# Layer 1: the network's first weight tiles fetched and split during the attention, and its first products in the steps of the last head group

## The chip, the core and the metric

The kernel runs on one core of one Trainium2 chip. The metric is the time of one execution on the device in microseconds (us), as the median of several runs. The engines are TensorE (PE; its weight loads are shown apart as PEld), VectorE (DVE), ScalarE (ACT), GpSimd (POOL) and SyncE (SP), which here only issues DMAs. Each works through a queue of its own in program order and waits on semaphores for the others.

## What is computed

Two transformer layers in float32 over S = 1024 tokens of width 512. The case touches only layer 1, and of it the end of the attention and the feed-forward network; both read the same normalised input `xn`:

```python
xn = _layernorm(x)
# grouped attention: H = 32 query heads of 16, G = 8 groups of 4 heads share keys and values
scores = einsum('bhqd,bhkd->bhqk', q, k); causal; weights = softmax(scores / sqrt(HD))
ctx = einsum('bhqk,bhkd->bhqd', weights, v)
attn = dot(ctx, Wo) + bo
# network: F = 2048
h = gelu(einsum('bsd,df->bsf', xn, inter_w) + inter_b, approximate=True)
out = einsum('bsf,fd->bsd', h, output_w) + output_b
x = x + attn + out
```

## The kernel before

**Products of float32 accuracy.** Most large products are made as three products of a faster type (`mm3`, lines 105 to 107): each operand is split into a high part (a cast by ACT) and a low part (operand less high part, a subtraction by POOL or DVE), and PE adds high x high, high x low and low x high into one PSUM bank. PSUM has 8 banks of 512 columns, `ps[:, 0]` to `ps[:, 7]`.

**Attention, `grouped_attention`.** Eight head groups g = 0 to 7, each of 12 steps (`STEPS`): four for the first 512 queries, eight for the last 512, one for each block of 128 keys. The width of a step is the number of queries that may look at the block: 512, 384, 256, 128, then 512 five times, 384, 256, 128. In a step PE makes the transposed scores of two pairs of heads (`keys`, line 1914, two products each, banks 0-1 and 2-3). ACT takes the exponential of each pair into `ga_pt` (line 1994). On the diagonal POOL masks a block (line 2032), and two steps later PE multiplies with the values (`weigh`, line 1930, eight instructions into bank 7). The scores of a bank pair may be written only when the exponential before has read it. Beside this, in each step, PE makes score products of the *next* group (line 1891, banks 4 to 6), and DVE their row maxima (line 1974), which give the shift of the softmax. The last group has no next one, so in its steps these products are missing. ACT copies the context out of bank 7 twice in a group (line 2007). SP writes it to memory, reads back its sums (`csum`, line 1766) and the context (line 1769); DVE inverts the sums (line 1795), SP writes these out (line 1777) and loads them spread out over partitions with eight DMAs (line 1788); POOL scales the heads with them (line 1802).

**Network, `heads_and_ffn`.** A new stage behind a barrier of all engines, with semaphores set anew. 16 tiles k of 128 hidden features. For each tile SP loads 256 KB of weights (`first`, line 2081, a ring of RW = 4 tiles), ACT makes the high part (`high1`, line 2148), POOL the low part (`low1`, line 2195). PE makes two halves of 512 tokens, 4 x 3 products each (`up`, 24 products for a tile, banks 2 * (k % 2) + half), and ACT applies bias and gelu (line 2159). `up(k)` waits for the low part of its tile, and from k = 2 for the gelu that frees the bank. Then `down` multiplies with the second weights and with Wo, 20 times, into all eight banks, and DVE adds x.

The order of the queues at the start of this stage, written out by hand:

- SP: tiles 0 and 1, b1, tiles 2 and 3; then for the last head group the sums, the context, the two bias vectors spread over partitions, the inverted sums out, the eight spread loads; then tile 4 and the others, each when its place in the ring is free.
- ACT: high parts of tiles 0 and 1; wait for b1; then for each k the high part of tile k + 2 and the two gelus of tile k.
- POOL: low parts in order of k; behind that of tile 4 the sum of the two biases (line 2207) and eight additions of it to x (line 2210); behind that of tile 6 the scaling of the last heads.

```python
for k in range(NC):
    low1(k)
    if k == 4:
        pool.wait_ge(bias_in, START + 32)
        pool.tensor_tensor(bias[:, 0], bias[:, 0], bias[:, 1], ALU.add).then_inc(bias_done, 1)
        ...
        for t in range(ST):
            pool.tensor_tensor(x[:, t], x[:, t], bias[:, 0], ALU.add).then_inc(x_ready, 1)
```

`outputs_to_queries` is the stage ahead of the attention (projections of layer 1). It has a weight buffer `oq_w` of two tiles and high parts `oq_wh` of six blocks of 128 columns.

Of the kernel before, what the change touches and what calls it, by code (L numbers as in the profile page):

```python
# [13 lines left out]
P = 128  # L14
# [1415 lines left out]
def outputs_to_queries(nc, c, ps, ident, x, ctx_d, wvo_d, xnh, xnl, wq, wkv, qkd, v32, ctxn, raw, sums, qst, kst, q_in,  # L1430
                       k_in, strip, nmax, nT, first):
# [26 lines left out]
    with ExitStack() as st:  # L1458
        cf = Ctx(nc, st)
        w = cf.sb("oq_w", [P, 2, DT, P])  # L1460
        wh = cf.sb("oq_wh", [P, DT, NW], F32R)
# [26 lines left out]
        with nc.Block() as block:  # L1488
# [41 lines left out]
            @block.gpsimd  # L1530
            def _(pool):
                def low_block(n):
                    pool.wait_ge(wh_done, START + n + 1)
                    at = slice(BLOCKS[n] * P, (BLOCKS[n] + 1) * P)
                    pool.tensor_tensor(wl[:, :, at], w[:, n % 2], f32(wh[:, :, at]), ALU.subtract).then_inc(wl_done, 1)

                for half, k, s, u in steps:
                    pool.wait_ge(split_done[s], START + u + 1)
                    pool.tensor_tensor(ol_w[:, s], wr[:, s], f32(oh_w[:, s]), ALU.subtract).then_inc(wvl_done[s], 1)
                    if (half, k) in SPLIT_AT:  # L1540
                        low_block(SPLIT_AT[half, k])
                    if (half, k) == (0, 5):
                        pool.memset(v32[:, :, :, HD1:], 1.0).then_inc(ones_done, 1)
                    if (half, k) == (0, 7):
                        pool.memset(f32(kst[:, :, 1]), 0.0).then_inc(zero_b, 1)
                        pool.wait_ge(zero_b, START + 1)
                        pool.memset(f32(kst[KQ1:KQ1 + 2, :, 1]), 1.0).then_inc(zero_b, 1)
                        pool.wait_ge(zero_b, START + 2)
                        pool.memset(f32(kst[KQ1:KQ1 + 1, :, 1]), 0.0).then_inc(zero_b, 1)
                        pool.wait_ge(zero_b, START + 3)  # L1550

            @block.scalar
            def _(act):
# [9 lines left out]
                def high_block(n):  # L1563
                    act.wait_ge(w_in[n % 2], START + LANDED[n])
                    at = slice(BLOCKS[n] * P, (BLOCKS[n] + 1) * P)
                    act.copy(wh[:, :, at], w[:, n % 2]).then_inc(wh_done, 1)
# [128 lines left out]
            def _(pe):  # L1695
# [20 lines left out]
                def task(n):  # L1716
# [9 lines left out]
                    for k in range(DT):  # L1726
                        if kind == "T":
                            a1, a2 = slice(m * P, (m + 1) * P), slice(h * HALF, (h + 1) * HALF)
                            ins = mm3(pe, ps[:, n % 4, :], (wh[:, k, a1], wl[:, k, a1]), (xnh[:, k, a2], xnl[:, k, a2]),
                                      k == 0, k == DT - 1)  # L1730
                            if k == DT - 1:
                                ins.then_inc(done, 1)
                        else:
                            a1 = slice(m * P, (m + 1) * P)
                            ins = mm3(pe, ps[:, n % 4, 0:KD], (xnh[:, k, a1], xnl[:, k, a1]),
                                      (wh[:, k, D + KD:], wl[:, k, D + KD:]), k == 0, k == DT - 1)
# [67 lines left out]

def grouped_attention(nc, ps, ident, strip, qkd, raw_d, inv_d, v32, ctxn, qst, kst, q_in, k_in, rest, nmax, nT,
                      first):
# [26 lines left out]
    with ExitStack() as st:  # L1833
# [12 lines left out]
        with nc.Block() as block:  # L1846
            @block.sync
            def _(sp):
# [16 lines left out]
                for g in range(G1):  # L1865
# [7 lines left out]
                    if g + NB < G1:  # L1873
                        load(g + NB)
                store(G1 - 1, 1)

            @block.tensor
            def _(pe):
# [59 lines left out]
                for g in range(G1):  # L1938
                    done = lead
                    for s in range(NSTEP):  # L1940
                        ahead = g + 1 if s < NSTEP - LEAD else g + 2
                        first = done if s < NSTEP - LEAD else done - UNITS
                        units = range(first, first + SHARE[s]) if ahead < G1 else range(0)
# [3 lines left out]
                        for v in units[:one]:  # L1947
                            score(ahead, v)
                        keys(g, s, 1)
                        for v in units[one:two]:  # L1950
                            score(ahead, v)
# [4 lines left out]
                        for v in units[two:]:  # L1956
                            score(ahead, v)
# [28 lines left out]
            def _(act):  # L1986
# [22 lines left out]
                for g in range(G1):  # L2009
                    for s in range(NSTEP):  # L2010
# [6 lines left out]
                        if s == 3 + LAG:  # L2017
                            take_ctx(g, 0)
                take_ctx(G1 - 1, 1)

            @block.gpsimd
            def _(pool):
                for g in range(G1):
                    for s, (half, j) in enumerate(STEPS):
                        off, q0, q1 = span(half, j)
                        if q0 == j * P:
                            n = g * NSTEP + s
                            for p in range(2):
# [4 lines left out]
                                               channel_multiplier=-1, compare_op=ALU.is_ge, fill=0.0).then_inc(sel_done, 1)  # L2033
                    if g >= 3 and g % 2 == 1:
# [4 lines left out]
def heads_and_ffn(nc, ps, xnh, xnl, x, ctxn, raw_d, inv_d, rest, wo, bo, w1, b1_d, w2, b2_d, out_d):  # L2039
# [5 lines left out]
    with ExitStack() as st:  # L2045
        c = Ctx(nc, st)
        g = c.sb("t_g", [P, NC, S])
        w1r = c.sb("t_w1r", [P, RW, DT, P])
        w1h = c.sb("t_w1h", [P, RW, DT, P], F32R)
        w1l = c.sb("t_w1l", [P, RW, DT, P], F32R)  # L2050
# [7 lines left out]
        names = ("b1_in", "bias_in", "bias_done", "x_ready", "w1h_done", "w1l_done", "w2h_done", "w2l_done", "hidden",  # L2058
                 "h_done", "gh_done", "gl_done", "used", "summed", "x_done", "stored")
        (b1_in, bias_in, bias_done, x_ready, w1h_done, w1l_done, w2h_done, w2l_done, hidden, h_done, gh_done, gl_done,  # L2060
         used, summed, x_done, stored) = (c.sem("t_" + n) for n in names)
        w1_in, w2_in = c.sems("t_w1_in", RW), c.sems("t_w2_in", RW)
        w1_v = w1.rearrange("(k p) n -> p k n", p=P)

# [10 lines left out]
        with nc.Block() as block:  # L2075
            @block.sync
            def _(sp):
                def first(k):
                    if k >= RW:
                        sp.wait_ge(w1l_done, START + k - RW + 1)  # L2080
                    sp.dma_start(w1r[:, k % RW], w1_v[:, :, k * P:(k + 1) * P]).then_inc(w1_in[k % RW], 16)
# [7 lines left out]
                first(0)  # L2089
                first(1)  # L2090
                sp.dma_start(b1[:, :], b1_d.rearrange("(k p) -> p k", p=P), allow_slow_non_contiguous=True).then_inc(b1_in, 16)
                first(2)
                first(3)
                for half in (1,):
# [15 lines left out]
            def _(pe):  # L2110
                def up(k):
                    pe.wait_ge(w1l_done, START + k + 1)
                    for half in range(2):
                        tok = slice(half * HALF, (half + 1) * HALF)
                        if k >= 2:
                            pe.wait_ge(h_done, START + 2 * (k - 2) + half + 1)
                        for j in range(DT):
                            ins = mm3(pe, ps[:, 2 * (k % 2) + half, :], (w1h[:, k % RW, j], w1l[:, k % RW, j]),
# [18 lines left out]
                for k in range(NC):  # L2137
                    up(k)
# [4 lines left out]
            def _(act):  # L2143
                def high1(k):
# [3 lines left out]
                    act.copy(w1h[:, k % RW], w1r[:, k % RW]).then_inc(w1h_done, 1)  # L2148
# [7 lines left out]
                def activate(k):  # L2156
                    for half in range(2):
                        act.wait_ge(hidden, START + 2 * k + half + 1)
                        act.activation(g[:, k, half * HALF:(half + 1) * HALF], ps[:, 2 * (k % 2) + half, :],
# [13 lines left out]
                high1(0)  # L2173
                high1(1)
# [17 lines left out]
            def _(pool):  # L2192
                def low1(k):
                    pool.wait_ge(w1h_done, START + k + 1)
                    pool.tensor_tensor(w1l[:, k % RW], w1r[:, k % RW], f32(w1h[:, k % RW]), ALU.subtract).then_inc(  # L2195
# [7 lines left out]
                for k in range(NC):  # L2203
# [68 lines left out]
def two_layers(nc, ins, consts, out):  # L2272
# [9 lines left out]
    with ExitStack() as top:  # L2282
# [44 lines left out]
        with ExitStack() as layer1:  # L2327
# [9 lines left out]
            for name in ("raw_out", "sum_in", "ctx_in", "scale_in"):  # L2337
                rest[name] = ca.sems(name, 2)
            with ExitStack() as inner:
# [10 lines left out]
                                   v32, ctxn, rest["raw"], rest["sums"], qst, kst, q_in, k_in, strip, nmax, nT, first)  # L2350
                grouped_attention(nc, ps, ident, strip, qkd, raw_d, inv_d, v32, ctxn, qst, kst, q_in, k_in, rest, nmax,
                                  nT, first)
            heads_and_ffn(nc, ps, xnh, xnl, x, ctxn, raw_d, inv_d, rest, I("L1_attn_Wo"), I("L1_attn_bo"),
                          I("L1_ffn_inter_w"), I("L1_ffn_inter_b"), I("L1_ffn_output_w"), I("L1_ffn_output_b"),
                          out.rearrange("b s d -> (b s) d"))
# [44 lines left out]
```

## Time and profile before

| | us |
|---|---|
| median of 3 runs (lowest, highest) | 1831.37 (1830.39, 1832.53) |
| profiled execution, its time | 1834.29 |
| span of its instructions | 1832.3 |
| PE, DVE, ACT, POOL busy | 1680.1, 1086.0, 851.1, 706.1 |
| last head group, PE's first to last product | 1593.5 to 1617.7 |
| network, PE's first product | 1627.1 |
| end | 1832.3 |

Times in the trace count from the first instruction. A line of the timeline gives start, duration, engine, line of the kernel, operation and tiles, how many instructions were joined (x), and in brackets the idle time of the engine just before, with what ended it. Busy times of PE overlap at their ends, since products are pipelined. PEclk is the clock granted to PE as a share of 2.4 GHz; it has two levels, 1.00 and 0.50. ACT, POOL and DVE idle time costs nothing where PE is fed.

### The profile page before, as it was taken

The page shows a single profiled execution, that of the slowest core. Times are in us where ns is not written, and L with a number is a line of the kernel's source. Part 1 is how long each engine was busy: PE and PEld are TensorE (multiplying, and loading weights), DVE is VectorE, ACT ScalarE, POOL GpSimd, SP SyncE. Part 2 cuts the span into 40 slices and gives each one's busy share as a digit, 9 for nine tenths or more (in the row PEclk, how much of TensorE's full clock was granted, in tenths as well). Part 3 has the DMA queues.
Part 4 walks back from the last instruction along what each step waited for, and adds up shares of the span by engine and source line. Part 5 has one row for each costly group of instructions (what it writes and reads, how often), then busy time and mean ns, then how long its engine had stood idle before and what let it go on. Part 6 is the DMA issues. An engine that isn't in the chain of part 4 may idle for free. (4 is left out here: it accounts for less than half of the span.)

```text
span 1832.3 us, 27319 instructions
## 1 busy us (share of the span) xinstructions
PE 1680.1 (92%) x8938; PEld 1239.9 (68%) x8938; DVE 1086.0 (59%) x2465; ACT 851.1 (46%) x1608; POOL 706.1 (39%) x745
## 2 busy tenths in 40 slices
PE   6889995999978999999999999699989999979998
PEld 5578884888767666766666666377865555458887
DVE  3436668999627667777667777336657676400122
ACT  3545554443315555555545555344125565643321
POOL 1211112444646555566555565186001121234221
PEclk9999997999988999999999999899979999989999
DMA  9820002221100000000000000165432243132111
GB/s 253 268 89 23 23 19 60 61 63 28 47 32 5 17 17 17 32 17 17 17 17 17 33 17 12 46 207 172 147 47 54 57 82 63 38 96 64 40 49 50
DMA packets 108155, 110.48 MB, mean 60 GB/s; under 512 B 39008, under 2 KB 70208, under 8 KB 108032
## 3 DMA queue, kind: packets, MB, share of 16 engines
q1 hardware_dynamic: 103936, 101.58, 20.2%
q10 hardware_dynamic: 4096, 7.34, 1.1%
q8 instruction: 67, 1.10, 0.3%
q14 instruction: 56, 0.46, 0.1%
HBM read 81.34 MB, written 27.39 MB: 59 GB/s over the span
## 5 line engine op out<-in xcount | busy, mean ns | idle before, releaser
L1212 POOL TENSOR_SCALAR a_p<-a_p,a_rinv 128x640 f32<-128x640 f32 (+7 forms) x256 | 190.2, 745 | 174.5 <-DVE a_rinv L1138 173.4
L1169 ACT ACTIVATE a_p<-a_sm,a_nmax 128x640 f32<-128x640 f32 (+7 forms) x256 | 198.6, 777 | 106.1 <-DVE a_nmax L1130 103.3
L1130 DVE CUSTOM_DVE_ANT_0 a_sm<-ps,maskb 128x640 f32<-128x640 f32 (+7 forms) x256 | 192.7, 753 | 92.1 <-PE ps L1074 88.6
L1974 DVE CUSTOM_DVE_ANT_0 ga_sm<-ps,strip 128x640 f32<-128x640 f32 (+1 forms) x224 | 163.3, 755 | 83.2 <-PE ps L1891 81.6
L1994 ACT ACTIVATE ga_pt<-ps 128x1024 f32<-128x1024 f32 (+1 forms) x192 | 147.7, 809 | 106.5 <-PE ps L1914 105.7
L1086 PE MATMUL ps<-ident,a_p 128*128 128x128 f32 x1152 | 173.0, 276 | 12.1 <-DVE a_pt L1145 11.8
L1086 PEld LDWEIGHTS ps<-ident,a_p 128*128 128x128 f32 x1152 | 133.6, 141 | 34.9 <-DVE a_pt L1145 11.2
L1101 PE MATMUL ps<-a_pt,vst 128*64 128x512 f32 (+3 forms) x768 | 152.5, 507 | 1.9 <-DVE a_pt L1145 1.1
L2032 POOL TENSOR_SCALAR_AFFINE_SELECT ga_pt<-ga_pt 128x512 f32<-128x512 f32 x64 | 40.6, 635 | 287.1 <-ACT ga_pt L1994 287.1
L1181 ACT COPY a_pt<-ps 128x512 f32<-128x512 f32 x128 | 74.2, 580 | 164.8 <-PE ps L1086 109.6
L1074 PE MATMUL ps<-kh,lq_qh 128*128 128x512 f32 (+3 forms) x384 | 132.1, 398 | 14.1 <-DVE a_nmax L1130 10.0
L617 DVE SCALAR_TENSOR_TENSOR idx<-ix_r,ix_sgc,idx 128x256 f32<-128x256 f32 (+6 forms) x112 | 96.4, 881 | 64.6 <-ACT ix_r L585 64.6
L1891 PE MATMUL ps<-ga_kst,ga_qst 96*128 96x512 f32 x336 | 107.5, 387 | 21.9 <-DVE ga_nmax L1974 14.7
L1074 PEld LDWEIGHTS ps<-kh,lq_qh 128*128 128x128 f32 x384 | 64.8, 192 | 89.6 <-issue 53.3
L585 ACT ACTIVATE ix_r<-ps,ix_awc 128x256 f32<-128x256 f32 (+6 forms) x112 | 89.1, 797 | 78.3 <-PE ps L550 61.9
L1145 DVE COPY a_pt<-ps 128x128 f32<-128x128 f32 (+3 forms) x256 | 121.2, 474 | 1.0 <-PE ps L1086 0.9
L1891 PEld LDWEIGHTS ps<-ga_kst,ga_qst 96*128 96x128 f32 x336 | 58.3, 195 | 92.5 <-DVE ga_nmax L1974 61.6
L1074 PE MATMUL ps<-kh,lq_ql 128*128 128x512 f32 (+3 forms) x384 | 113.4, 350 | 0.0
L1074 PE MATMUL ps<-kl,lq_qh 128*128 128x512 f32 (+3 forms) x384 | 113.4, 350 | 0.0
L1301 POOL TENSOR_TENSOR lq_t<-lq_t 128x512 f32<-128x512 f32 x64 | 81.5, 1274 | 80.6 <-DVE lq_t L1296 80.6
L1914 PE MATMUL ps<-ga_qst,ga_kst 98*128 98x512 f32 (+3 forms) x384 | 102.6, 362 | 1.6 <-DMA ga_qst<-ga_nT 0.7
L2260 DVE MAX8 top<-idx 128x8 f32<-128x1024 f32 (+3 forms) x112 | 87.5, 816 | 4.9 <-DVE idx L2253 1.3
(279 smaller groups left out, 4039.7 us busy)
## 6 DMA issues: line engine op xcount, KB each, us to landing
op_wo<-in_L_attn_o_w SPq DMA_DIRECT2D x16, 512.0 KB, 6.5
ctx_d<-a_ctxst SPq DMA_DIRECT2D x16, 512.0 KB, 2.9
ctxn<-ctx_d SPq DMA_DIRECT2D x32, 256.0 KB, 3.6
ctxn<-wvo_d SPq DMA_DIRECT2D x32, 256.0 KB, 4.2
ga_qst<-qkd SPq DMA_DIRECT2D x42, 128.0 KB, 4.2
f_wr<-in_L_ffn_w SPq DMA_DIRECT2D x20, 256.0 KB, 2.6
op_wq<-in_L_attn_q_b_w SPq DMA_DIRECT2D x16, 288.0 KB, 5.2
x<-in_L_attn_hidden_states SPq DMA_DIRECT2D x16, 256.0 KB, 4.3
```

The costliest lines, as they stand in the source:

```text
L617: dve.scalar_tensor_tensor(out=acc, in0=r[:, u % 2, 0:W], scalar=sgc[:, a, t:t + 1], in1=acc, op0=ALU.mult, op1=ALU.add).then_inc(added[u ...
L1074: ins = pe.matmul(slots[kind][:, k0:k1], l[:, a, at], r[:, k0:k1], start=j == 0, stop=j == 2, skip_group_check=True)
L1086: ins = pe.transpose(ps[:, bank_t[n % NT], k * P:(k + 1) * P], p[kind][:, v // 2 % 2, (j0 + k) * P:(j0 + k + 1) * P], qwork["ident"][:, :])
L1101: ins = pe.matmul(ps[64 * a:64 * a + 64, bank_c, off:HALF], vst[:, j, :], pt[half][:, (2 * i + a) % NBUF, j, off:HALF], start=j == 0, stop ...
L1130: dve.tensor_tensor_reduce(out=sm[kind][:, 0:w], in0=slots[kind][:, 0:w], in1=maskb[:, MASK_OFF[t]:MASK_OFF[t + 1]], scale=-scale, scalar= ...
L1145: dve.tensor_copy(pt[g][:, buf, j0:j0 + m, at], bank4(ps, bank_t[n % NT])[:, 0:m]).then_inc(pt_done[n % NT], 1)
L1169: act.activation(p[kind][:, v // 2 % 2, 0:w], sm[kind][:, 0:w], ACT.Exp, bias=nmax[:, v % 4:v % 4 + 1], scale=-1.0, accum_out=rsum[:, v % ...
L1212: pool.tensor_scalar(mine, mine, rinv[:, v % 4:v % 4 + 1], 1.0, ALU.mult, ALU.mult).then_inc(norm_done, 1)
L1891: ins = pe.matmul(slots[kind][:, k0:k1], qst[0:KQ, b, h // 2, t * P:(t + 1) * P], kst[0:KQ, b, h % 2, k0:k1], start=True, stop=True)
L1914: ins = pe.matmul(ps[:, 2 * p + a, 0:q1 - q0], kst[0:KQ + 2, b, a, j * P:(j + 1) * P], qst[0:KQ + 2, b, p, q0:q1], start=True, stop=True)
L1974: dve.tensor_tensor_reduce(out=sm[kind][:, 0:w], in0=slots[kind][:, 0:w], in1=strip[:, S - w:], scale=-1.0, scalar=3.0e38, op0=ALU.add, op ...
L1994: act.activation(pt[:, n % RING, 2 * p:2 * p + 2, off:HALF], ps[:, 2 * p:2 * p + 2, 0:q1 - q0], ACT.Exp, scale=SCALE).then_inc(exp_done[p], 1)
```

## The change

Buffers for two weight tiles with their high and low parts (`ahead`: `r`, `h`, `l`) and their semaphores live through all of layer 1. In the stage before the attention they serve as the weight buffer and as four of the six blocks of high parts, so that no memory is added there. During the attention SP loads tiles 0 and 1 in group 5 (behind the scales of group 4), ACT makes their high parts in group 6 behind the exponentials of steps 5 and 7, and POOL their low parts behind the masks of group 6. In the last group (7) PE makes one `mm3` (3 products) at the end of each of the 12 steps, into banks 4, 5 and 6: both halves of tile 0 and the first half of tile 1. In the network's stage `up` begins at tile 1, second half, into bank 7; tiles 2 and 3 take banks 0 to 3 and no longer wait for a gelu; SP begins with tiles 2 and 3 and b1; ACT begins with the wait for b1; POOL begins with the low part of tile 2. The rest of the queues is as it was.

```diff
@@ grouped_attention, SP
                     if g + NB < G1:
                         load(g + NB)
+                    if g == G1 - 3:
+                        for k in range(2):
+                            load_first(sp, ahead, w1, k)
@@ grouped_attention, PE, at the end of each step
+                        if g == G1 - 1:
+                            k, n = divmod(s, 2 * DT)
+                            if n == 0:
+                                pe.wait_ge(ahead["low"], START + k + 1)
+                            half, i = divmod(n, DT)
+                            at = slice(half * HALF, (half + 1) * HALF)
+                            ins = mm3(pe, ps[:, 4 + 2 * k + half, :], (ahead["h"][:, k, i], ahead["l"][:, k, i]),
+                                      (xnh[:, i, at], xnl[:, i, at]), i == 0, i == DT - 1)
+                            if i == DT - 1:
+                                ins.then_inc(ahead["hidden"], 1)
@@ grouped_attention, ACT
                         if s == 3 + LAG:
                             take_ctx(g, 0)
+                        if g == G1 - 2 and s in (5, 7):
+                            split_first(act, ahead, (s - 5) // 2)
@@ grouped_attention, POOL
+                    if g == G1 - 2:
+                        for k in range(2):
+                            low_first(pool, ahead, k)
                     if g >= 3 and g % 2 == 1:
                         scale_heads(pool, g // 2 - 1, ctxn, rest)
@@ heads_and_ffn
+        def bank(k, half):
+            return 2 * (k % 2) + half + (4 if k < 2 else 0)
@@ heads_and_ffn, SP
-                first(0)
-                first(1)
-                sp.dma_start(b1[:, :], ...)
                 first(2)
                 first(3)
+                sp.dma_start(b1[:, :], ...)
@@ heads_and_ffn, PE
-                    for half in range(2):
+                    for half in range(1 if k == 1 else 0, 2):
-                        if k >= 2:
+                        if k >= 4:
                             pe.wait_ge(h_done, START + 2 * (k - 2) + half + 1)
...
-                for k in range(NC):
+                for k in range(1, NC):
                     up(k)
@@ heads_and_ffn, ACT
-                high1(0)
-                high1(1)
                 act.wait_ge(b1_in, START + 16)
@@ heads_and_ffn, POOL
-                for k in range(NC):
+                for k in range(2, NC):
                     low1(k)
```

The new functions do what their counterparts in the network's stage do:

```python
def load_first(sp, ahead, w1, k):
    sp.dma_start(ahead["r"][:, k], w1.rearrange("(k p) n -> p k n", p=P)[:, :, k * P:(k + 1) * P]).then_inc(ahead["in"][k], 16)

def split_first(act, ahead, k):
    act.wait_ge(ahead["in"][k], START + 16)
    act.copy(ahead["h"][:, k], ahead["r"][:, k]).then_inc(ahead["high"], 1)

def low_first(pool, ahead, k):
    pool.wait_ge(ahead["high"], START + k + 1)
    pool.tensor_tensor(ahead["l"][:, k], ahead["r"][:, k], f32(ahead["h"][:, k]), ALU.subtract).then_inc(ahead["low"], 1)
```

## Rows read from the trace of the kernel before

**Rows 1.** Page, chain that ended last: shares of the span by line.

```profile
PE ps L105 4%; PE ps L106 4%; PE ps L107 4%; DMA t_w1r<-in_L_ffn_inter_w 0%; POOL t_w1l L2195 0%; DVE x L2226 0%; ACT t_w1h L2148 0%
```

**Rows 2.** Timeline, start of the network: start, us, engine, line, op, tiles, xcount [idle before].

```profile
1621.02 0.96 SPq L2081 DMA_DIRECT2D t_w1r<-in_L_ffn_inter_w  x2
1622.03 1.76 SPq L2091 DMA_DIRECT2D t_b<-in_L_ffn_inter_b  x1
1623.83 2.32 SPq L2081 DMA_DIRECT2D t_w1r<-in_L_ffn_inter_w  x2
1625.10 0.62 ACT L2148 CAST t_w1h<-t_w1r 128x512 fp32r<-128x512 f32 x1 [6.71 <-DMA t_w1r<-in_L_ffn_inter_w]
...
1626.20 1.89 SPq L1766 DMA_DIRECT2D csum<-raw_d  x4
1627.11 0.79 PE L105 MATMUL ps<-xnh,t_w1h 128*128 128x512 f32 x1 [9.37 <-POOL t_w1l L2195]
...
1637.56 2.08 SPq L2081 DMA_DIRECT2D t_w1r<-in_L_ffn_inter_w  x4
```

**Rows 3.** Windows: length, busy PE, PEld, DVE, ACT, POOL (count), PEclk, DMA share, GB/s.

```profile
1593.50:1617.75 24.25, 23.14 (x160) 9.49 (x160) 0.35 (x1) 18.82 (x26) 5.90 (x10) 1.00 0.22 54
1619.50:1620.00 0.50, 0.00 (x0) 0.00 (x0) 0.00 (x0) 0.00 (x0) 0.00 (x0) 0.66 0.92 344
1627.00:1634.00 7.00, 6.89 (x18) 5.41 (x19) 0.35 (x1) 2.59 (x3) 2.57 (x3) 0.55 0.54 149
```

**Rows 4.** Timeline, POOL in the network's stage, low parts of tiles 4 to 6.

```profile
1642.51 1.29 POOL L2195 TENSOR_TENSOR t_w1l<-t_w1r,t_w1h 128x512 fp32r<-128x512 f32 x1 [4.15 <-ACT t_w1h L2148]
...
1645.13 10.08 POOL L2210 TENSOR_TENSOR x<-x,t_bias 128x512 f32<-128x512 f32 x8
1655.17 2.53 POOL L2195 TENSOR_TENSOR t_w1l<-t_w1r,t_w1h 128x512 fp32r<-128x512 f32 x2
```

**Rows 5.** Timeline, ACT: second gelus of tiles 4 and 5.

```profile
1657.56 0.69 ACT L2159 ACTIVATE t_g<-ps,t_b 128x512 f32<-128x512 f32 x1 [2.03 <-PE ps L107]
...
1663.00 0.69 ACT L2159 ACTIVATE t_g<-ps,t_b 128x512 f32<-128x512 f32 x1 [2.03 <-PE ps L107]
```

**Rows 6.** Timeline, PE in the last head group: `keys` (L1914) and `weigh` (L1930).

```profile
1599.94 0.85 PE L1930 MATMUL ps<-ga_pt,v 128*32 128x384 f32 x8
...
1600.72 1.20 PE L1914 MATMUL ps<-ga_qst,ga_kst 98*128 98x512 f32 x4
...
1609.31 1.20 PE L1914 MATMUL ps<-ga_qst,ga_kst 98*128 98x512 f32 x4
...
1610.44 1.07 PE L1930 MATMUL ps<-ga_pt,v 128*32 128x512 f32 x8
...
1613.61 0.74 PE L1914 MATMUL ps<-ga_qst,ga_kst 98*128 98x256 f32 x4
...
1614.28 1.06 PE L1930 MATMUL ps<-ga_pt,v 128*32 128x512 f32 x8
...
1615.28 0.66 PE L1914 MATMUL ps<-ga_qst,ga_kst 98*128 98x128 f32 x4
...
1615.87 1.28 PE L1930 MATMUL ps<-ga_pt,v 128*32 128x384 f32 x16
```

**Rows 7.** Timeline: ACT in step 8 of group 6; POOL's first mask of group 7.

```profile
1584.83 1.94 ACT L1994 ACTIVATE ga_pt<-ps 128x1024 f32<-128x1024 f32 x2 [0.95 <-PE ps L1914]
...
1596.34 0.63 POOL L2032 TENSOR_SCALAR_AFFINE_SELECT ga_pt<-ga_pt 128x512 f32<-128x512 f32 x1 [2.59 <-ACT ga_pt L1994]
```

**Rows 8.** DMA issues and landings: inverted sums (1592, 1630), b1, tile 4's load (1637.6).

```profile
inv_d<-csum SPq DMA_DIRECT2D x2, 8.0 KB, 1.5
...
inv_d<-csum SPq DMA_DIRECT2D x2, 8.0 KB, 3.4
...
DMA to landing us min/median/max: 4.7/4.7/4.7
...
DMA to landing us min/median/max: 3.0/3.0/3.0
```

More of the change, by code:

```diff
@@ L1430, in outputs_to_queries @@
 def outputs_to_queries(nc, c, ps, ident, x, ctx_d, wvo_d, xnh, xnl, wq, wkv, qkd, v32, ctxn, raw, sums, qst, kst, q_in,
-                       k_in, strip, nmax, nT, first):
+                       k_in, strip, nmax, nT, first, ahead):
     NS = 4
@@ L1459, in outputs_to_queries @@
         cf = Ctx(nc, st)
-        w = cf.sb("oq_w", [P, 2, DT, P])
-        wh = cf.sb("oq_wh", [P, DT, NW], F32R)
+        w = ahead["r"]
+        wh_more = cf.sb("oq_wh", [P, 2, DT, P], F32R)
+        wh = [t[:, k] for t in (ahead["h"], ahead["l"], wh_more) for k in range(2)]
         wl = cf.sb("oq_wl", [P, DT, NW], F32R)
@@ L1940, in _ @@
                     for s in range(NSTEP):
-                        ahead = g + 1 if s < NSTEP - LEAD else g + 2
+                        later = g + 1 if s < NSTEP - LEAD else g + 2
                         first = done if s < NSTEP - LEAD else done - UNITS
-                        units = range(first, first + SHARE[s]) if ahead < G1 else range(0)
+                        units = range(first, first + SHARE[s]) if later < G1 else range(0)
                         done += SHARE[s]
@@ L1947, in _ @@
                         for v in units[:one]:
-                            score(ahead, v)
+                            score(later, v)
                         keys(g, s, 1)
                         for v in units[one:two]:
-                            score(ahead, v)
+                            score(later, v)
                         if s == NSTEP - LEAD and g + 1 < G1:
@@ L1956, in _ @@
                         for v in units[two:]:
-                            score(ahead, v)
+                            score(later, v)
+                        if g == G1 - 1:
[8 more added lines that the diff above has]
+                                ins.then_inc(ahead["hidden"], 1)
                 for s in range(NSTEP - LAG, NSTEP):
@@ L2036, in grouped_attention, with heads_and_ffn @@
         c.finish()
[L2039 removed]
+def heads_and_ffn(nc, ps, xnh, xnl, x, ctxn, raw_d, inv_d, rest, wo, bo, w1, b1_d, w2, b2_d, out_d, ahead):
     NC = F1 // P
@@ L2047, in heads_and_ffn @@
         g = c.sb("t_g", [P, NC, S])
-        w1r = c.sb("t_w1r", [P, RW, DT, P])
-        w1h = c.sb("t_w1h", [P, RW, DT, P], F32R)
-        w1l = c.sb("t_w1l", [P, RW, DT, P], F32R)
+        w1r_more = c.sb("t_w1r", [P, 2, DT, P])
+        w1h_more = c.sb("t_w1h", [P, 2, DT, P], F32R)
+        w1l_more = c.sb("t_w1l", [P, 2, DT, P], F32R)
+        w1r, w1h, w1l = ([t[:, k] for t in pair for k in range(2)] for pair in (
+            (ahead["r"], w1r_more), (ahead["h"], w1h_more), (ahead["l"], w1l_more)))
         w2r = c.sb("t_w2r", [P, RW, D])
@@ L2338, in two_layers @@
                 rest[name] = ca.sems(name, 2)
+            ahead = dict(r=ca.sb("ah_r", [P, 2, DT, P]), h=ca.sb("ah_h", [P, 2, DT, P], F32R),
+                         l=ca.sb("ah_l", [P, 2, DT, P], F32R), high=ca.sem("ah_high"), low=ca.sem("ah_low"),
+                         hidden=ca.sem("ah_hidden"))
+            ahead["in"] = ca.sems("ah_in", 2)
             with ExitStack() as inner:
```

38 lines of the change are left out of this document (19 added, 19 removed).

## The prediction

> **What bounds the kernel now.** Read first the chain of work that ended last [rows 1]: followed back from the last instruction it is TensorE (PE) nearly alone, by three lines, 105 to 107, the three products of `mm3`, and it stops at the load of the network's first weight tile. So from that load to the end PE sets the time, and what the change gains or loses must be read where PE is *not* yet fed. Second, the timeline around the start of the last stage [rows 2]: SP issues the tile's load at 1621.02 (call this moment T0 in both kernels); PE starts at 1627.11 after 9.37 us of idle, so its last product of the attention ended at 1617.74. Third, the last head group by itself [rows 3]: 24.25 us with PE at 23.14 and ScalarE at 18.82, so PE there has little room. Fourth, GpSimd (POOL) after the seam [rows 4]: this queue turns out to decide.
>
> **Into the last head group: 36 products.** One `mm3` in each of 12 steps. Their price when fed is a gelu pitch of 5.44 us per tile of 24 products [rows 5], so 0.227 us each and 8.15 us in all. What hides them is only PE's waiting. From the code the 12 steps have widths 512 (six), 384, 256 and 128 (two each). Four score products (`keys`) take from their start to the start of `weigh` 1.13 us at width 512, 0.67 at 256, 0.59 at 128 [rows 6], and I put 0.90 for 384: 6.78 + 1.80 + 1.34 + 1.18 = 11.1 us. `weigh` takes 0.99 us at 512 and 0.78 at 384 [rows 6], a slope of 0.21 per 128 columns, so 0.57 and 0.36 below. Fourteen run in this stretch (two belong to the group before): 6 x 0.99 + 2 x 0.78 + 3 x 0.57 + 3 x 0.36 = 10.3 us. PE work 21.4 of 24.25 us: 2.85 us is waiting for exponentials. With the products added a wide step costs 1.13 + 0.99 + 0.68 = 2.80 us on PE against 1.94 us of ScalarE's two exponentials, so PE binds nearly every step and the waiting is used up. **Growth 8.15 - 2.85 = 5.3; with 0.1, an estimate, for the two steps in which ScalarE also copies the context, 5.4 us.** Bounds: 8.15 if nothing hides; 4.5 if the switches between kinds of product overlap too.
>
> **Edits costed at nothing.** The two loads go out on SP in the sixth group behind the scales; 256 KB each, and one group (some 25 us) passes before they are used. ScalarE's two splits of 0.61 us stand in the seventh group behind the exponentials of steps 5 and 7; what is queued behind them are exponentials that wait for PE anyway (0.95 us of idle before the one after step 7 [rows 7]); without that cover 1.2 us. POOL's two subtractions (1.27 us each) come behind the seventh group's last mask, which ends at 1593.75 (its successor starts at 1596.34 after 2.59 us of idle [rows 7]), so they end near 1595.1 and 1596.4. PE's new wait for the first one comes at about 1593.5 + 1.13 + 0.57 = 1595.2, after `weigh` of that step, and finds it just done; behind it stand the next step's `keys` and so ScalarE. The first mask of the last group, queued behind both, is wanted at 1596.3: late by 0.1, and its reader comes 2 us later. Zero, and 1.3 us if one of the two is late. The reused banks 4 to 6 are idle in the last group, since no maxima are left.
>
> **At the seam.** In before PE sits from 1617.7 to 1627.1. Now it can start at about T0 with the 12 products that tile 1 lacks. The granted clock falls to half (1.2 GHz) about 2 us after PE's last product [rows 3], before T0, so these take 5.1 us (the starts of products lie 0.427 apart behind 1627.11, 18 of them in 7 us with the last ones faster [rows 3]), to T0+5.1. Then tile 2 is wanted. ScalarE first waits for b1: in before that load goes out at T0+1.0 and lands 4.7 us later [rows 2, 8]; its place is the same. Split 0.62 [rows 2] and subtraction 1.27 [rows 4]: tile 2 is ready at T0+7.7. A new wait of 2.6 us, but far better than before, where the same work would be reached at 1627.1 plus two tiles. Were nothing else late, the tail would gain 6.1 (idle) + 8.15 (products gone) - 2.6 = 11.7 us.
>
> **What is late next.** Tile 4's load stands on SP behind the whole chain of the last group's sums: four loads of sums, context, two biases, the inverted sums out, their return, eight broadcasts. It went out at 1637.56 = T0+16.5 [rows 2]. The chain starts (1626.20) when SP has issued its five first loads; two of them are gone. The one after b1 took most of 2.32 us for two (normal 0.5 each), which I read as b1's small pieces holding the queue, and that delay passes to the next load. So the chain starts earlier by 1.2 us (bounds 0 and 2.4) and tile 4's load goes at T0+15.4. Landing 3.0 us as in before [rows 8], split 0.65: its subtraction starts at T0+19.0, ends T0+20.3. Tiles 2 and 3, 48 products, partly at half clock, keep PE until T0+21, so tile 4 is just in time; tile 4 ends at T0+26.4.
>
> Then POOL. Its order is not changed: behind tile 4's subtraction stand the bias sum and eight additions to x, and only then tile 5's subtraction. From the start of the one (1642.51) to the start of the other (1655.17) is 12.66 us [rows 4], all of it POOL's own work. In before this was hidden: tile 5's subtraction ended at 1656.44 and PE reached tile 5 at 1657.40, 1.0 us of slack (gelu of tile 4's second half at 1657.56 [rows 5]). Now tile 5 is ready at 19.0 + 12.66 + 1.27 = T0+33.0 while PE wants it at T0+26.4: **a stall of 6.6 us**. PE starts tile 5 at T0+33.0 against T0+36.4 before: a gain of only 3.35 us. All after that is 11 tiles at 5.44 us in both.
>
> **The clock.** A PE idle of 6.6 us is longer than the one of 3.3 us (1617.7 to 1621.0) in which the granted clock fell. After the restart at 1627.11 it stayed at half until 1633.3: mean 0.55 over 7 us [rows 3] is 6.3 us at half, a loss of 3.1 us. The same loss is due again at tile 5; the one at the seam now lies inside time that the POOL chain covers. **3.1 us (bounds 0 and 3.4).**
>
> **Sum.** +5.4 (group) - 3.35 (tile 5 earlier) + 3.1 (clock) = +5.2 us. The profiled execution has a span of 1832.3 and a time of 1834.29, 2.9 us over the median of the three runs, 1831.37; nothing of that difference lies in the stages touched, so I add the 5.2 to the median: **1836.6 us**.
>
> The Trainium skill (DMA: Bandwidth & Descriptors, Latency and other measured facts) says that the fixed cost of a small transfer is mostly the memory's round trip and shrinks with lighter load. The rows agree in direction: the inverted sums landed in 1.5 us in an ordinary group and in 3.4 at the seam [rows 8]. By that rule, with two weight tiles less in flight, tile 4's load would come up to 1.9 us earlier still; this is rival A.
>
> **Rivals.**
> A, not slower: the chain of sums on SP shortens more. If the inverted sums land in 1.5 us instead of 3.4 and SP's full 2.4 us is saved, tile 4's load goes at T0+12.3 and tile 5 starts at T0+29.9, 6.5 us earlier than before. PE's idle is then 3.5 us. Net 5.4 - 6.5 + 3.1 = +2.0, or -1.1 where the clock holds: 1830.3 to 1833.4, within 0.2%. It decides from a load of tile 4 before T0+14. Against it: both bias broadcasts (256 KB each) still go out just ahead of the inverted sums.
> B, clearly faster: POOL doesn't hold tile 5 (its additions overlap with what they should block). Then 11.7 of gain less 5.4: 1825.1. Against it speaks the queue's order, which is in the code and in [rows 4].
> C, slower still: the last group hides nothing, 8.15 instead of 5.4, as when a product of one kind behind one of another drains first or a low part comes late at step 0: 1839.3; with the chain of sums not shortened, 1840.5.
> That the change doesn't do what it says would need PE to wait at the seam as before; the early splits exclude it.
>
> **Chances.** Forecast 0.52, A 0.22, B 0.07, C 0.19. The range takes in A and most of C: 1830.3 to 1841.0. A measurement of this kernel tells about 0.2% (3.7 us) from no change. The forecast's own spread (terms of about 1 us each) puts some 0.1 of its 0.52 under 1835.0: faster 0.07, same 0.31, slower 0.62.
>
> **What would show it.** Last group (first to last product) 29.6 us instead of 24.25; PE's first product of the network at T0, at half clock; a wait of about 2.6 us for tile 2; POOL's eight additions starting at about T0+21.7; the longest PE wait of the tail, 6 to 7 us, on POOL's subtraction for tile 5, and the clock at half behind it. Wrong would be: no PE wait before tile 5 (B), tile 4's load before T0+14 (A), or a group over 31 us (C).

## The result, and the profile after

| | before | changed |
|---|---|---|
| median us (22 runs each) | 1831.3 | 1836.1 |
| lowest, highest us | 1827.8, 1837.7 | 1831.4, 1842.9 |
| ratio, 95% interval | | 1.0025 (1.0016 to 1.0035) |
| profiled execution: time, span | 1834.3, 1832.3 | 1835.4, 1833.2 |
| first score of the last group | 1593.51 | 1590.70 |
| from there to the end | 238.8 | 242.5 |

The change makes the kernel 0.25% slower: 4.8 us by the medians, 2.9 to 6.4 by the interval. 1836.6 was forecast.

The spans differ by 0.9 us only, because in this execution the changed kernel came to the last group 2.8 us earlier. That lies in stages the change leaves alone: in before the clock was at half for 3.4 us from 1169 on and for 27.3 us from 1340 on, in the changed kernel not at all at the first place and for 23.9 us at the second. Such differences appear from run to run of these kernels, and the single times go with them: of the changed kernel's 22 runs, the four under 1833.5 us had a mean granted clock of 0.968 to 0.970, the three over 1841 us 0.963 to 0.965. So the parts are compared below **from the first score product of the last group to the end**: +3.8 us in the two profiles (238.75 and 242.51).

The chain of the changed kernel, from its page, is no longer nearly PE alone. POOL's additions to x, SP's issues and the inverted sums now stand in it; compare [rows 1]:

```profile
PE 9%; POOL 1%; SPq 1%; DMA 0%; issue 0%; DVE 0%; ACT 0%
PE ps L105 3%; PE ps L106 3%; PE ps L107 3%; POOL x L2247 1%; DMA inv_d<-csum 0%; SPq L1788 0%; SPq L1766 0%; DMA ah_r<-in_L_ffn_inter_w 0%; POOL ah_l L2232 0%; POOL t_bias L2244 0%; SPq L2122 0%; DVE x L2263 0%; ACT ah_h L2187 0%; SPq L1769 0%; SPq L2132 0%
```

Its waits between 1620 and 1720 (who waited for what: us in total, times, longest) name the place: PE waits for low parts of POOL, once for 6.7 us, and once 2.2 us for tile 2.

```profile
ACT ah_h L2187 <- DMA ah_r<-in_L_ffn_inter_w: 8.3, 1, 8.3
...
PE ps L105 <- POOL ah_l L2232: 7.2, 2, 6.7
...
PE ps L105 <- PEq L70: 2.4, 1, 2.4
PE ps L105 <- POOL t_w1l L2232: 2.2, 1, 2.2
```

Timelines of the changed kernel, to be laid beside [rows 2] and [rows 4]. T0 is 1623.22. SP's chain of sums starts at T0+1.5 instead of T0+5.2, but its four small loads take 3.38 us to issue instead of 1.89, and the second of the two transfers of inverted sums lands 4.6 us after its issue, against 3.6 in before; tile 4's load goes at T0+15.2:

```profile
1623.22 0.95 SPq L2122 DMA_DIRECT2D t_w1r<-in_L_ffn_inter_w  x2
1624.22 0.50 SPq L2132 DMA_DIRECT2D t_b<-in_L_ffn_inter_b  x1
1624.76 3.38 SPq L1766 DMA_DIRECT2D csum<-raw_d  x4
...
1629.74 0.90 SPq L1777 DMA_DIRECT2D inv_d<-csum  x2
1634.79 3.57 SPq L1788 DMA_DIRECT2D sums<-inv_d  x8
1638.41 0.98 SPq L2122 DMA_DIRECT2D ah_r<-in_L_ffn_inter_w  x2
```

The DMA view of the changed kernel (KB of one, median us from issue to landing) for the inverted sums and the bias load just ahead of them, issued at 1629.27:

```profile
t_bias<-in_L_ffn_output_b SPq DMA_DIRECT2D x1, 256.0 KB, 5.1
inv_d<-csum SPq DMA_DIRECT2D x2, 8.0 KB, 4.1
```

POOL makes tile 4's low part, the bias sum and eight additions without a pause, then tile 5's low part:

```profile
1641.93 1.29 POOL L2232 TENSOR_TENSOR ah_l<-ah_r,ah_h 128x512 fp32r<-128x512 f32 x1 [8.84 <-ACT ah_h L2187]
1643.17 1.29 POOL L2244 TENSOR_TENSOR t_bias<-t_bias 128x512 f32<-128x512 f32 x1
1644.54 9.91 POOL L2247 TENSOR_TENSOR x<-x,t_bias 128x512 f32<-128x512 f32 x8
1654.42 1.26 POOL L2232 TENSOR_TENSOR ah_l<-ah_r,ah_h 128x512 fp32r<-128x512 f32 x1
```

The stretches of the changed kernel (columns as in [rows 3]): the last group, the wait before tile 5, and what follows it, again at half clock:

```profile
1590.50:1620.90 30.40, 30.06 (x196) 16.37 (x196) 0.35 (x1) 18.93 (x27) 9.31 (x12) 1.00 0.19 46
...
1649.00:1655.70 6.70, 0.01 (x1) 0.00 (x0) 0.00 (x0) 1.19 (x2) 6.70 (x7) 0.89 0.00 0
1655.70:1662.00 6.30, 6.27 (x17) 4.94 (x18) 0.00 (x0) 0.69 (x1) 4.78 (x3) 0.58 0.35 101
```

A step of the last group, in full width (`keys` L1934, `weigh` L1950), against [rows 6]; the next `keys` start at 1612.84, so it takes 2.81 us:

```profile
1610.03 1.09 PE L1934 MATMUL ps<-ga_qst,ga_kst 98*128 98x512 f32 x4
1611.05 1.07 PE L1950 MATMUL ps<-ga_pt,v 128*32 128x512 f32 x8
1612.05 0.50 PE L105 MATMUL ps<-xnh,ah_h 128*128 128x512 f32 x1
...
1612.84 0.86 PE L1934 MATMUL ps<-ga_qst,ga_kst 98*128 98x384 f32 x4
```

### The profile page after: what moved, and what is told of

It reads as the page before. It is cut to its first block and busy times, and to the rows that moved or that the text cites. A ratio compares the mean times of both kernels' runs of the same rounds, so it can differ in the third digit from the quotient of the medians.

```text
span 1833.2 us, 27317 instructions
## 1 busy us (share of the span) xinstructions
PE 1679.7 (92%) x8938; PEld 1238.1 (68%) x8938; DVE 1078.4 (59%) x2465; ACT 850.3 (46%) x1608; POOL 704.6 (38%) x745
## 5 line engine op out<-in xcount | busy, mean ns | idle before, releaser
L1934 PE MATMUL ps<-ga_qst,ga_kst 98*128 98x512 f32 (+3 forms) x384 | 100.0, 357 | 1.1 <-DMA ga_qst<-ga_nT 1.1
```

The costliest lines, as they stand in the source:

```text
L1934: ins = pe.matmul(ps[:, 2 * p + a, 0:q1 - q0], kst[0:KQ + 2, b, a, j * P:(j + 1) * P], qst[0:KQ + 2, b, p, q0:q1], start=True, stop=True)
```

## The experiments

All were timed against the kernel before, with 12 runs each (e9 8, e10 6, e11 9). "Length" is from the first score of the last group to the end, in the one profiled execution, as a difference of two readings of its trace; the clock's state further up doesn't enter it. What differs between executions behind that point does: before and e2, the same kernel but for an edit without effect, differ by 0.2 us, but the load of b1 and the clock at T0 moved some lengths by 1 to 2 us, as said at e4 and e11.

| kernel | median us | ratio to before (95%) | length us | tile 5 starts |
|---|---|---|---|---|
| before | | | 238.8 | T0+36.4 |
| changed | 1836.1 | 1.0025 (1.0016, 1.0035) | 242.5 | T0+32.5 |
| e1 additions spread | 1827.9 | 0.9977 (0.9962, 0.9993) | 232.7 | no wait |
| e2 before, spread | 1830.9 | 1.0003 (0.9988, 1.0019) | 239.0 | no wait |
| e3 tiles only | 1832.0 | 1.0004 (0.9989, 1.0019) | 237.2 | T0+32.8 |
| e4 PE kept busy | 1832.3 | 1.0012 (0.9998, 1.0025) | 241.5 | T0+33.9 |
| e5 tile 4 ahead | 1828.0 | 0.9978 (0.9962, 0.9993) | 233.7 | T0+26.1 |
| e6 products twice | 1837.3 | 1.0022 (1.0008, 1.0036) | 242.1 | T0+32.6 |
| e7 spread, high parts first | 1827.7 | 0.9988 (0.9971, 1.0005) | 232.9 | no wait |
| e8 the same, tiles only | 1826.4 | 0.9974 (0.9958, 0.9989) | 232.4 | no wait |
| e9 products in the gap | 1821.2 | 0.9941 (0.9920, 0.9963) | 227.9 | no wait |
| e10 gap and waits | 1821.8 | 0.9927 (0.9905, 0.9950) | 226.4 | no wait |
| e11 e7 with tile 4 ahead | 1823.9 | 0.9947 (0.9928, 0.9966) | 228.8 | no wait |

Kernels of one row of four (e1 to e4, e5 to e8, e9 to e11) shared a chip; across these groups the ratios compare, not the medians.

### Is it POOL's queue that holds tile 5?

**e1**, the changed kernel, and **e2**, the kernel before, with the same edit on POOL:

```diff
-                    if k == 4:
+                    if k == 8:
                         pool.wait_ge(bias_in, START + 32)
                         pool.tensor_tensor(bias[:, 0], bias[:, 0], bias[:, 1], ALU.add)...
-                        for t in range(ST):
-                            pool.tensor_tensor(x[:, t], x[:, t], bias[:, 0], ALU.add)...
+                    if k >= 8:
+                        t = k - 8
+                        pool.tensor_tensor(x[:, t], x[:, t], bias[:, 0], ALU.add)...
```

> The changed kernel with one edit on POOL: the bias sum and the eight additions to x no longer stand behind the low part of tile 4, but one behind each of the low parts of tiles 8 to 15. Theory (POOL's queue holds tile 5): the wait before tile 5 (6.7 us in the changed kernel's trace) goes, since tile 5's low part follows tile 4's and is ready near T0+21.5, before PE asks at T0+25.8; the half clock behind it (2.6 us) goes with it. 9.3 us faster than the changed kernel: 1826.8 us, so faster than before by 4.5. Rival 1 (the change is slower because of the products in the last group or because of more traffic, whatever POOL does): within 1 us of the changed kernel, 1835 to 1837. Rival 2 (SP's chain is next, tile 4 or 5 comes late in another way): between, about 1831, with a wait of PE on a load.

> The kernel before with the same edit on POOL alone. Theory: POOL's additions were hidden there (tile 5's low part ended 1.0 us before PE came to it), so the time stays within 0.5 us, 1831.3. Rival (the additions cost something in themselves, as by contention with PE, DVE or ScalarE): 2 us or more faster also here, and then the gain of the same edit on the changed kernel is not the wait.

The edit takes the changed kernel from 1.0025 to 0.9977 of before (two sets of runs), some 8.8 us, and 9.8 us off its length; on before it does nothing (1.0003; 239.0 against 238.8). Of PE's waits in e1 between 1594 and 1720 only these are left, both at the seam:

```profile
PE ps L105 <- PEq L70: 2.4, 1, 2.4
PE ps L105 <- POOL t_w1l L2232: 2.2, 1, 2.2
```

So the additions are harmless where PE comes late, and in the changed kernel their place ahead of tile 5 turns a gain of 0.2% into a loss of 0.25%.

### What is in front of POOL's queue?

**e5**, the changed kernel with two loads moved on SP:

```diff
+                first(4)
+                first(5)
                 spread_scales(sp, G1 - 1, inv_d, rest)
-                for k in range(4, NC):
+                for k in range(6, NC):
                     first(k)
```

> The changed kernel with one edit on SP: the loads of tiles 4 and 5 go out ahead of the inverted sums and the eight spread loads instead of behind them; POOL's order stays. Theory (the chain that holds tile 5 is SP's sums, then tile 4, then POOL's 12.5 us): tile 4's low part is ready near T0+12 instead of T0+20, the additions end near T0+24, tile 5 near T0+25, just before PE asks for it at T0+25.8. The wait of 6.7 us and the half clock behind it go: 9.3 us faster than the changed kernel, 1826.8, or 2 us less of that if the biases land late. Rival (only POOL's own work counts, the position of the load doesn't): within 1 us of the changed kernel.

0.9978; length 233.7, 8.8 less than the changed kernel. POOL's block takes 12.6 us as before, but starts at 1638.07, T0+12.2 (T0 is 1625.87), and PE waits 1.09 us for tile 5 instead of 6.7:

```profile
1638.07 1.29 POOL L2234 TENSOR_TENSOR ah_l<-ah_r,ah_h 128x512 fp32r<-128x512 f32 x1 [2.34 <-ACT ah_h L2189]
1639.33 1.29 POOL L2246 TENSOR_TENSOR t_bias<-t_bias 128x512 f32<-128x512 f32 x1
1640.69 10.05 POOL L2249 TENSOR_TENSOR x<-x,t_bias 128x512 f32<-128x512 f32 x8
1650.68 1.28 POOL L2234 TENSOR_TENSOR ah_l<-ah_r,ah_h 128x512 fp32r<-128x512 f32 x1
```

Both links of the chain, SP's order and POOL's, are shown: to break either is enough.

### Is the clock the third term?

**e4**, the changed kernel with 27 products for nothing ahead of tile 5:

```diff
                 for k in range(1, NC):
+                    if k == 5:
+                        for _ in range(27):
+                            pe.matmul(ps[:, 4, :], xnh[:, 0, 0:P], xnh[:, 0, 0:HALF], start=True, stop=True)
                     up(k)
```

> The changed kernel with 27 extra products of 128x512 (6.1 us at full clock) put before tile 5, on operands that are ready, into a bank that is free; their result is overwritten. Theory: they lie in the wait of 6.7 us for POOL, the clock stays full and tile 5 runs at full pace: 2.6 us faster than the changed kernel, 1833.5, with the granted clock at 1.00 behind tile 5's start. Rival (the wait is not one on POOL, or what is lost behind it is not the clock): not faster, or up to 6 us slower.

The stretch behind tile 5's start, 0.58 in the changed kernel, is at full clock here:

```profile
1646.00:1654.50 8.50, 7.72 (x35) 6.09 (x34) 0.00 (x0) 1.20 (x2) 8.50 (x8) 1.00 0.00 0
1654.50:1661.00 6.50, 6.50 (x29) 5.38 (x30) 0.00 (x0) 1.59 (x3) 4.62 (x3) 1.00 0.36 103
```

From tile 5's start to the end it takes 175.0 us, as before does (174.9), the changed kernel 177.5: the half clock is worth 2.5 us. The whole is only 1.1 shorter in length, since tile 5 came 1.4 us later in this execution: b1's load took 2.27 us to issue instead of 0.50, tile 4's load went at T0+16.4 instead of T0+15.2, and PE waited 3.7 us for tile 2 instead of 2.2. The ratios (1.0012 against 1.0025) differ by 2.4 us, but their intervals overlap, so it is the trace that shows the 2.5 us.

### The tiles without the products

**e3** drops the products from the group (`up` makes tiles 0 and 1 whole):

```diff
-                        if g == G1 - 1:
-                            ... the mm3 of each step
...
-                    for half in range(1 if k == 1 else 0, 2):
+                    for half in range(2):
...
-                for k in range(1, NC):
+                for k in range(NC):
```

> The changed kernel without its products in the last group: tiles 0 and 1 are loaded and split during the attention, but PE makes all their 48 products in the network's stage. Theory: the group takes 24.2 us as before; PE starts at T0, reaches the end of tile 4 at about T0+30.2 and waits 2.3 us for tile 5 (ready at T0+32.5, set by SP's chain and POOL's additions). Tile 5 starts 3.9 us earlier than in before; the clock holds through so short a wait. 3.9 us faster than before: 1827.4; 1830.4 if the clock falls. Rival (the early tiles themselves cost the time, by their loads, splits and subtractions in groups 5 to 7): as slow as the changed kernel, 1835 to 1837.

A miss: no gain by the times (1.0004), 1.6 us in length. Tile 5 does start earlier, 60.8 us behind the group's first score instead of 63.9. But the clock fell in a wait of 2.9 us, which I had thought too short, and gave 1.6 of it back. PE's first product of tile 5 in the timeline:

```profile
1649.37 0.80 PE L105 MATMUL ps<-xnh,ah_h 128*128 128x512 f32 x1 [2.88 <-POOL ah_l L2222]
```

and the window behind it (columns as in [rows 3]):

```profile
1649.00:1653.00 4.00, 3.63 (x10) 2.90 (x11) 0.00 (x0) 0.00 (x0) 4.00 (x4) 0.57 0.43 128
```

That also rules out the early loads, splits and subtractions as the cause of the loss: the group takes 24.2 us with them.

**e6** makes the 36 products in the group without use; the network's stage makes them again:

```diff
-                            if i == DT - 1:
-                                ins.then_inc(ahead["hidden"], 1)
```

(on e3, with the `mm3` of each step kept.)

> As the kernel with the early tiles alone (expected at 1827.4), but with the 36 products in the last group made for nothing: the network's stage makes them again. The difference to that kernel is the price of the products in the group. Theory: the group grows by 5.9 us as in the changed kernel's trace, the gap between the group and T0 shrinks by 0.9: 5.0 us slower than the kernel with the early tiles alone, 1832.4. Rival (nothing is hidden): 8.2 to 9.4 us slower. Rival (products disturb what follows, too): more than 10.

4.9 us longer than e3 in length (242.1 against 237.2), by the ratios 3.3 (1.0022 against 1.0004, in two sets of runs). The group takes 30.2 us, the gap to T0 2.4 instead of 3.8 us (in e3 SP was late with its last loads of sums, and T0 came 0.5 us later than in before). Of the 4.9 us, 4.6 lie ahead of T0. So the price of the products in the group is confirmed apart from what follows, to within the half microsecond by which T0 moves.

### What does the change bring once nothing stands in its way?

**e7** is e1 with the high parts of tiles 2 and 3 ahead of ScalarE's wait for b1; **e8** the same without products in the group.

```diff
+                high1(2)
+                high1(3)
                 act.wait_ge(b1_in, START + 16)
                 for k in range(NC):
                     if k + 2 < NC:
-                        high1(k + 2)
+                        if k > 1:
+                            high1(k + 2)
```

> The changed kernel with POOL's additions spread over tiles 8 to 15, and ScalarE's high parts of tiles 2 and 3 ahead of its wait for b1. Theory: 9.3 us faster than the changed kernel by the first edit; by the second tile 2 is ready 0.8 us earlier (at about T0+6.0 instead of T0+6.8) and PE's wait for it is 0.9 us. 1826.0. Rival: the second edit does nothing, 1826.8.

> The same two edits on the kernel without products in the last group. Theory: PE runs from T0 without a wait, tile 5 starts at T0+30.2 instead of T0+36.4: 6.2 us faster than before, 1825.1. Against the kernel with the products in the group this tells whether these pay at all: they take 8.2 us out of the tail, add 5.0 to group and gap, and leave a wait of some 0.9 for tile 2. By that they should win by 2 us; by the sums of both from the kernel before the two are within 1 us of each other.

e8 (0.9974; 232.4) is no worse than e7 (0.9988, an interval that reaches over 1; 232.9) or e1. With these two edits the products in the steps bring nothing over the early tiles alone. e7 is 0.2 longer than e1: tile 2 was ready at T0+5.0, even earlier than the T0+6.0 expected, but PE then waited 2.2 us for tile 4, whose load still stood behind the inverted sums. **e11** moves that load too (the edit of e5):

> The changed kernel (36 products in the steps) with all three edits on the other queues: additions spread, high parts of tiles 2 and 3 first, tiles 4 and 5 loaded ahead of the inverted sums. In the kernel with the first two, PE waited 2.15 us for tile 4, whose load stood behind the inverted sums. Theory: that wait goes, 2.1 us faster than that kernel (232.85 us from the group's first product to the end, now 230.7), 1825 to 1826. Rival (the clock at T0 decides instead): no difference.

228.8 instead of 232.9, 0.9947: twice the gain expected. 2.2 us are the wait; the rest fits the clock, which was at half for 3.4 us in both: in e7 from T0+5.0 on, so that it slowed tile 2, in e11 from T0+0.3 to T0+3.7, over before tile 2 began at T0+4.9, so that it only shortened PE's wait for tile 2. That part differs from execution to execution.

e11 corrects the reading of e7: with tile 4's load moved as well, the products in the steps do pay, by 3.6 us of length over e8. The kernel e8 with that load moved was not run, but e8 has no PE wait behind T0 (none over 0.1 us in the trace) that the move could take away.

**e9** and **e10** put the products elsewhere, with all three edits. e9 makes no product in the steps, but 12 behind the group's last `weigh`, where PE has nothing to do until T0; e10 makes those of the second half there, and those of the first in the four steps in which `keys` had waited for ScalarE, between its two pairs (the last two added lines, which e9 lacks):

```diff
                 for s in range(NSTEP - LAG, NSTEP):
                     weigh(G1 - 1, s)
+                for i in range(DT):
+                    ins = mm3(pe, ps[:, 4, :], ...)
...
                         keys(g, s, 0)
+                        if g == G1 - 1 and s in (1, 5, 6, 9):
+                            ins = mm3(pe, ps[:, 4, :], ...)
                         keys(g, s, 1)
```

> Early tiles, additions spread, high parts of tiles 2 and 3 ahead of the wait for b1, tiles 4 and 5 loaded ahead of the inverted sums; and the products stand elsewhere: none in the steps of the last group, 12 (tile 0, first half) behind its last product, where PE is otherwise idle for 3 us until T0. Theory: the group stays at 24.2 us, the 12 products (2.7 us at full clock) fill the gap, T0 moves by 0 to 0.8 us, and PE's idle before T0 is under 1.5 us, too short for the clock to fall, so the 3 us lost at half clock behind T0 go as well. Against the kernel with early tiles and spread additions (1826.4 measured): 2.7 - 0.5 + 3 = 5 us faster, 1821.3; from the group's first product to the end 227 us instead of 232.4. Rival (the clock falls all the same, or the barrier waits for PE): 0 to 2 us faster.

> As the one with 12 products in the gap, and 12 more in the last group, only in steps 1, 5, 6 and 9, between the two pairs of scores, where PE waited 0.3 to 0.6 us for ScalarE in the kernel before. Theory: each set costs 0.7 us of which 0.3 to 0.5 is waiting, so the group grows by about 1.0 us and the tail loses 2.7: 1.7 us faster than the kernel with the gap alone, 1819.6, and 225.5 us from the group's first product to the end. Rival (as in the changed kernel, what is put into the group costs nearly what it saves): the same time as the kernel with the gap alone.

e9 is 0.6% faster than before, with a third of the change's products. Its length of 227.9 is 4.4 us below e8's. T0 comes 28.5 us behind the group's first score against 27.5 in before and 27.3 in e8, so the 12 products delay the barrier by 1.2 us against e8; PE's idle before T0 is 1.3 us. The clock stays full through the seam, where e8 has PE at half clock for 6.1 us behind T0, 3.1 us of work lost. 2.7 + 3.1 - 1.2 = 4.6, near the 4.4. Against e11, with all 36 products in the steps, e9 is 0.8 us shorter in one profile each, and in the times (0.9941 and 0.9947) the two can't be told apart. PE's last products of the attention stage, PE's wait at T0, and the window around both (1608 to 1625):

```profile
1616.89 0.39 PE L105 MATMUL ps<-xnh,ah_h 128*128 128x512 f32 x1
1617.12 0.39 PE L106 MATMUL ps<-xnl,ah_h 128*128 128x512 f32 x1
1617.35 0.39 PE L107 MATMUL ps<-xnh,ah_l 128*128 128x512 f32 x1
```

```profile
PE ps L105 <- PEq L70: 1.3, 1, 1.3
```

```profile
1608.00:1625.00 17.00, 15.52 (x98) 9.73 (x91) 0.00 (x0) 7.77 (x13) 7.32 (x7) 1.00 0.33 72
```

e10's group grows by 1.1 us for 12 products worth 2.7, its length falls by another 1.6. In the times e9 and e10 can't be told apart (0.9941 and 0.9927, both intervals wide).

## Why the prediction was right, step by step

- **The group.** Forecast +5.4, measured +5.9 (30.12 against 24.23). Most steps came within 0.05 us (2.81 for 2.80 at full width); steps 0, 2 and 6 came 0.12 to 0.18 us over it and account for 0.4; what held them is not shown, PE's waits there are under 0.1 us each. The step's sum was right with wrong parts: the three products took 0.80 us instead of 0.68, wide `keys` 1.01 instead of 1.13. The 0.1 us falls on whatever stands behind `weigh`: it was in the price of `keys` and passed to the new products. They weren't free: 36 cost 5.9 of their 8.15 us.
- **The gap to T0.** Not in the sum: 2.4 us instead of 3.3, so -0.9. In before POOL was the last to reach the barrier, with the heads' scaling of 2.35 us behind its last mask; PE's new products run beside it.
- **The seam.** PE starts at T0, as said. The clock was not yet at half there: it fell at T0+0.3, for 3.4 us, and again at T0+7.1 behind the wait for tile 2, for another 3.4. Tile 2 was ready at T0+6.8 instead of 7.7: b1 landed in 3.8 us, not 4.7. All this is off the path, since the POOL chain covers it.
- **Tile 4's load.** Forecast T0+15.4, measured T0+15.2: luck, from two errors that cancel. SP reached the context load 2.1 us earlier than in before instead of 1.2: the delay behind b1 did pass to the next load, as assumed (the first of the sums' loads took 1.99 us to issue), but b1 itself took 0.50 instead of 1.76. That is no merit of the new order: b1's issue took 0.50 in e2, with the old order, and 2.27 in e4, with the new one, where tile 4's load went at T0+16.4. Against that the inverted sums took a median of 4.1 us to land instead of 3.4. The rule of the Trainium skill weighed there (DMA: Bandwidth & Descriptors, Latency and other measured facts: less load, smaller fixed cost) would have made them faster, but the load on them was no lighter: in before the last of the four weight tiles had landed at 1628.9, ahead of their issue at 1630.0. What was in flight in both kernels are the two bias loads, and the inverted sums land right behind the second of them (1634.41 and 1634.77 in the changed kernel, 1633.59 and 1633.94 in before). The prediction had named these two loads as what speaks against rival A, in which the sums land in 1.5 us; it is out.
- **POOL.** 12.49 us from tile 4's low part to tile 5's, forecast 12.66; tile 5 at T0+32.5, forecast T0+33.0; PE came to it at T0+25.8, forecast T0+26.4, so that the wait is 6.7, forecast 6.6. e1 and e5 show the cause. Rival B fell by the queue's order.
- **The clock.** Forecast 3.1, measured 2.6 in the changed kernel (177.5 - 174.9), and 2.5 by e4.
- **Sum.** +5.9 - 0.9 - 3.9 + 2.6 = +3.7 (3.8 unrounded) in the profiles, +4.8 in the medians, +5.2 forecast. The term left out (the gap, -0.9), the earlier tile 5 (-0.5) and the clock (-0.5) pull one way, the group (+0.5) the other. The mechanism is the forecast one, but by the profiles the sum is 1.4 us too high; that the medians come within 0.5 of it is in part luck, with an interval from 2.9 to 6.4. Rival C was nowhere needed.

## What to carry to other kernels

When work is taken off the start of a stage, every queue of that stage is asked earlier: list for each tile when it is wanted and when it is ready, before and after, and look for slack that is smaller than the shift (here tile 5 had 1.0 us of slack, and PE asked for it 10.6 us earlier). Work without a deadline, like the additions to x, belongs behind the work with one; moved there it cost nothing (e2). And a cheap place for spare products is the gap at a barrier, where they also kept the clock up: with the queues cleared, 12 products there brought as much as 36 in the steps of a nearly full engine.

## What the runs showed of the hardware

- How short an idle may be for the granted clock to hold is not one number. PE's idle of 2.4 us at T0 was followed by half clock in the changed kernel, e1, e4, e5 and e11 (0.3 to 1.3 us behind T0) and in e7 (5.0 us behind T0, at the end of another wait of 1.9 us), but not in e6. 2.9 us was enough in e3. 1.3 us (e9, e10), 1.1 us (e5) and 0.8 us (e4) never were. Half clock then lasted 3.4 us behind idle of 1.9 to 2.9 us (and behind e4's 3.7), 6.8 us with idle of 3.1 (e8), 3.8 (e3), 5.1 (e6) and 6.7 us, and 13.7 us around before's 9.4 us.
- A load of 2048 single elements (b1) holds up SP's queue, by its own issue or by that of the next DMA. The next one took 1.77 us to issue in before (a weight tile), 1.99 in the changed kernel (a 2 KB load of sums) and 3.61 in e2, against some 0.5 otherwise. b1's own took 0.50 to 2.27 us. Both together took 2.4 to 4.1 us over the 13 profiles, and that spread moves all that stands behind them on the queue.
- A small transfer did not overtake a large one ahead of it on the queue: in all 13 profiles the second transfer of inverted sums (8 KB, 3.6 us and more to land) landed 0.34 to 0.37 us behind the last 256 KB load issued ahead of it, however long that had taken. In before the same transfer landed in 1.5 us at 1592, with no such load just ahead [rows 8], and in 3.4 us at 1610, behind the 128 KB load of the context.
- The first product of full width behind eight of `weigh` took 0.33 us from start to start, the next ones 0.23 (1612.05, 1612.38, 1612.61 in the changed kernel).
- The clock's state upstream shifts single executions by several us. With 12 runs the ratio's interval is some 3 us to either side; lengths inside the trace told effects of 2 to 3 us apart, once the load of b1 and the clock at T0 were looked at beside them.
